# A pair's second masks made one slot later, and the next adjacency loaded behind the rows

## What is computed

```python
mask = adjacency + eye > 0                      # first network, the same for its 3 layers
for l in range(3):
    scores = leaky(si[:, :, None] + sj[:, None, :] + attn_b[l])
    attn = softmax(where(mask, scores, -inf))
    h = layernorm(x + attn @ x)
    x = layernorm(h + gelu(h @ W1[l] + b1[l]) @ W2[l] + b2[l])
# second network, 8 heads: the mask is adjacency > 0
att = softmax(where(A > 0, leaky(a_src + a_dst + b), NEG_INF))
out = relu(att @ xh)
```

## Time and profile before

| | |
|---|---|
| median of 3 runs | 2313.42 us (2313.23 to 2313.54) |
| the profiled execution, its own time | 2312.53 us |
| span from its first to its last instruction | 2310.8 us |
| TensorE busy (matmul) | 2213.7 us, 96% of the span |
| VectorE busy | 1809.3 us, 78% |
| ScalarE busy | 1684.7 us, 73% |
| mean granted TensorE clock | 0.985 of full |

### The profile page before, as it was taken

How to read it: one execution, slowest core, us unless ns; L and a number is a source line. 1 busy time by engine, 2 the same in 40 slices (tenths; PEclk the granted TensorE clock), 3 DMA queues, 4 the chain that set the end, 5 groups by cost and what they waited for, 6 DMA issues and landing times.

```text
span 2310.8 us, 32320 instructions
## 1 busy us (share of the span) xinstructions
PE 2213.7 (96%) x10501; PEld 1560.7 (68%) x10501; DVE 1809.3 (78%) x5722; ACT 1684.7 (73%) x3243; POOL 201.1 (9%) x200
## 2 busy tenths in 40 slices
PE   5999999999999999999999999999999999999976
PEld 3766767767766777676676667766776776777643
DVE  5566687878788788887788797887878877766777
ACT  2444468777877768777787778787787877888786
POOL 0010110010100110001100101000100011001100
PEclk9999999999999999999999999999999999999978
DMA  6011025333172242432353430632415322200111
GB/s 221 10 37 55 10 96 158 106 115 124 28 219 87 74 142 78 155 124 65 109 154 97 137 119 29 203 107 73 135 53 184 110 64 93 69 19 19 37 42 37
DMA packets 115874, 219.30 MB, mean 95 GB/s; under 512 B 7768, under 2 KB 57212, under 8 KB 110332
## 3 DMA queue, kind: packets, MB, share of 16 engines
q1 hardware_dynamic: 115708, 217.24, 29.8%
HBM read 164.52 MB, written 52.69 MB: 94 GB/s over the span
## 4 chain that ended last, share of the span: by engine, by line
PE 79%; DVE 13%; ACT 4%; issue 2%; POOL 1%; DMA 0%; DVEq 0%; POOLq 0%; ACTq 0%
PE ffn L1246 22%; PE av L1163 14%; PE ffn L1235 12%; PE av L1235 12%; PE pT L1146 9%; PE av L1187 4%; PE av L1222 2%; DVE prob L778 2%; DVE prob L769 1%; ACT xs L553 1%; POOL rstd L470 1%; DVE lone L730 1%; PE trow L1125 1%; PE av L1273 1%; PE trow L1273 1%
## 5 line engine op out<-in xcount | busy, mean ns | idle before, releaser
L1246 PE MATMUL ffn<-w_sb,G 128*128 128x256 f32 x3072 | 740.5, 381 | 0.0
L1246 PEld LDWEIGHTS ffn<-w_sb,G 128*128 128x128 f32 x3072 | 560.8, 191 | 90.2 <-issue 24.3
L778 DVE CUSTOM_DVE_ANT_0 prob<-trow,mask 128x512 f32<-128x512 f32 x676 | 439.0, 685 | 34.3 <-PE trow L1125 19.5
L1146 PEld LDWEIGHTS pT<-ident,prob 128*128 128x128 f32 x2032 | 256.4, 144 | 147.6 <-issue 101.5
L1235 PE MATMUL ffn<-hT,w_sb 128*128 128x512 f32 x768 | 355.0, 595 | 0.9 <-issue 0.9
L1235 PE MATMUL av<-hT,w_sb 128*128 128x512 f32 x768 | 353.8, 593 | 0.0
L470 POOL TENSOR_TENSOR rstd<-veps,mhalf 128x4 f32<-128x4 f32 x127 | 167.2, 1317 | 2071.9 <-DVE veps L713 2071.9
L513 ACT ACTIVATE prob<-prob,s 128x512 f32<-128x512 f32 x484 | 331.5, 715 | 2.4 <-DVE nm L785 1.8
L1146 PE MATMUL pT<-ident,prob 128*128 128x128 f32 x2032 | 312.3, 278 | 19.8 <-DVE prob L841 7.5
L519 ACT ACTIVATE prob<-prob,nm 128x512 f32<-128x512 f32 x448 | 317.6, 712 | 0.0
L1163 PE MATMUL av<-xs,prob 128*128 128x257 f32 x1024 | 244.3, 380 | 3.9 <-ACT prob L524 3.9
(11 more groups left out here) (154 smaller groups left out, 2727.2 us busy)
## 6 DMA issues: line engine op xcount, KB each, us to landing
w_sb<-in_L_gnn_W SPq DMA_DIRECT2D x48, 1024.0 KB, 8.4
blocks_dram<-blocks SPq DMA_DIRECT2D x168, 256.0 KB, 4.2
prob<-blocks_dram SPq DMA_DIRECT2D x42, 1024.0 KB, 4.8
trow<-rows_dram SPq DMA_DIRECT2D x127, 256.0 KB, 3.2
adj_sb<-in_adj SPq DMA_DIRECT2D x16, 1024.0 KB, 7.0
xin<-in_x SPq DMA_DIRECT2D x16, 512.0 KB, 6.2
x0r<-in_x SPq DMA_DIRECT2D x16, 512.0 KB, 5.8
out<-o SPq DMA_DIRECT2D x15, 512.0 KB, 3.2
```

What stands on the lines that cost most here:

```text
L778: return v.tensor_tensor_reduce(out=out_[:, t, :], in0=targets, in1=mask[:, t, :], scale=1.0, scalar=LEAST, op0=ALU.add, op1=ALU.max, accu ...
L1146: last = te.transpose(pT[bank][:, j * P:(j + 1) * P], src[:, t, j * P:(j + 1) * P], ident[:])
L1246: last = te.matmul(ffn[part][:, at:at + D], G[:, f, t * P:(t + 1) * P], w2_sb[:, g // 2 % STAGES, f, :], start=f == 0, stop=f == FT - 1)
```

## The change

`make_masks(1)` leaves the end of the slot k = 5. It is called in slot k = 0 of the next pair, between the scores (and `heads_out`, where there is one) and `first_targets`. In seven slots, those with k = 0 and p from 1 to 7, it thus stands directly ahead of the first instructions that read the mask. The masks of the very first pair are made ahead of the loop, as before. On the queue of SyncE, the wait for s_masks and the load of the next pair's first adjacency leave the head of the slot k = 0 and stand behind both x loads, the weights and the rows of the slot's second head.

```diff
                 if k == 0 and not last:
-                    sp.wait_ge(s_masks, 2 * p + 2)
-                    load_adj(2 * p + 2)
                     sp.wait_ge(s_av0e, (SLOTS * p + 1) * T)
                     load_x(2 * p + 2)
...
                 for q in new[1:2]:
                     load_rows(q + 1)
+                if k == 0 and not last:
+                    sp.wait_ge(s_masks, 2 * p + 2)
+                    load_adj(2 * p + 2)
...
                 if four is not None:
                     heads_out(four)
+                if k == 0 and p:
+                    make_masks(1)
                 first_targets(s2)
...
                 if k == SLOTS - 1:
                     keep_masks(1)
-                    if p < PAIRS - 1:
-                        make_masks(1)
```

## The result

The changed kernel takes 2353.49 us (median of 4 runs, 2352.40 to 2354.38), the kernel before 2313.32 us beside it; the ratio is 1.0176 with a 95% interval of 1.0160 to 1.0192. It is slower by 40.2 us, inside the range and 4.5 us above the forecast. The profiled execution took 2352.40 us with a span of 2350.6 us, which is 39.8 more than before.

What follows compares the result with a forecast made beforehand. The prediction took TensorE, busy 96% of the span, as the bound. It summed 2312.53 + 28.7 (masks on the chain) + 7.4 (clock) = 2348.6 us, the median 0.9 above, and said 2349, range 2340 to 2361.

Steps and rivals of the forecast that it cites:

- The price of the old place: Masks ending k = 5 delay the closing sum, so TensorE's row of targets is 0.75 us late in six slots: 4.6 us.
- the rival (c): VectorE's idle time takes up the masks and only the gain is left: 2308.8 us; chance 0.04.
- The masks on the chain: In k = 0, g = 12 to 42, s_nm0 comes 3.76 us later (6.38 less 2.62): 22.6 us over six slots.
- Both waits of TensorE: In the six slots, 3.3 us before piece 3 for the eighth gelu, then some 1.2 us for the first probability.
- Slot 6: Nothing is won ahead of it; s_nm0 is 6.3 us later, of which 6.1 us arrive.
- Nothing gives it back: Behind the new waits no TensorE idle time in slot 18 recovers the loss; VectorE and ScalarE shift with it.
- The clock: TensorE's clock falls around the new waits: 0.8 us in each of six slots, 2.6 in slot 6, 7.4 us in all.
- stretches of 0.50 behind each of these waits: Sign expected in the profile: TensorE's granted clock at 0.50 behind each of line 1246's seven waits, 3.3 and 5.5 us.
- The rival (a): TensorE's clock does not fall, because work surrounds the waits: 2342.1 us; chance 0.18.
- (b): Clock falls are long, two to three lengths in every slot, 18 to 28 us: 2360 to 2370 us; chance 0.11.
- The queue: On SyncE the adjacency load moves about 30 us later; its reader comes over two slots later, so cost is nothing.
- (d): Change does not act as written, for instance masks wait for the adjacency or the queue stands: above 2360 us; chance 0.03.

Runs made afterwards that it cites:

- the kernel without masks: Changed kernel without make_masks(1) in the loop, later second graphs using graph 1's masks, waits and loads kept: 2307.12 us, ratio 0.9973 to the kernel before.
- the filler: Changed kernel plus eight unread matmuls (3.4 us) in front of piece 3 in slots k = 0 behind the first pair: 2343.50 us.
- both single halves: Two kernels: the changed kernel with SyncE's old queue order, 2353.04 us; the kernel before with only the adjacency load moved behind the rows, 2312.73 us.
- The split kernel: Changed kernel with the masks cut in two, 3.9 us at the end of k = 5, 2.5 us ahead of the targets: 2317.14 us.
- the gelu ahead: Changed kernel with ScalarE's eighth gelu ahead of all four scores in slots k = 0 behind the first pair: 2340.59 us.
- the version that beats both: Kernel before, masks in place, but their adjacency reduction done early at the ends of k = 0 and k = 4: 2302.13 us, ratio 0.9953.

## Why the prediction was right, point by point

**The price of the old place** was put at 0.75 us in each of six slots. The direction was right, the size a bit small: without the masks slot 18 takes 45.3 us, 1.0 less than before. The wait at line 1125 isn't all that a late start costs: the row of targets started 12.1 us into the slot before and 11.2 without the masks, 0.9 apart, `attend` 22.1 and 21.1. The view's idle time understates such a delay, since it counts from the modelled end of a matmul group, which reaches over the start of the next (1.88 us long, the next 1.72 behind its start). So the bound of the rival (c), 2308.8, was too high by some 1.5 us, and the 2307.1 of the kernel without masks lies below it. In the sum of the prediction the 0.75 doesn't count by itself: it went by the chain, 6.38 - 2.62.

**The masks on the chain** were put at 6.38 - 2.62 = 3.76 us later for s_nm0. Measured: 20.43 - 16.43 = 4.0, and six slots of 50.3 for 46.3, 24 us for the predicted 22.6. The duration of the masks was right (848.88 to 855.22, 6.3). What was left out is small: from the masks' first instruction to the targets it is 6.56 us for 6.38, since `first_targets` waits 0.21 us behind the masks' last instruction, a result of its own engine; and the closing sum starts 0.28 behind TensorE's next slot instead of 0.20. Both waits of TensorE are where they were said to be: 3.71 for 3.3, 0.79 for 1.2, 4.5 together as predicted. The 0.79 shows only in the two slots at full clock; in the others slower work fills it.

**Slot 6**: 6.1 predicted. With its clock's share taken off it is an estimated 6.3: 47.7 (with the filler), less 1.6 (a fall at its end, which in the kernel without masks cost 41.4 - 39.8), less 39.8.

**Nothing gives it back**: right. The slots k = 1, 2, 3 and 5 from slot 7 on have the length they had.

**The clock** was put at 7.4 us, 0.8 for each of the six and 2.6 for slot 6. Measured in the seven slots against the filled ones: 7.1. The spread was not right: 1.7, 0, 1.9, 0, 1.9 and 0.6 in the six, 6.0 in all for the 4.8 predicted, and 1.1 in slot 6 for 2.6. In slot 6 the fall had the 6.8 us that were forecast, but half of it lay over idle time: TensorE was busy for 3.36 of the 6.80 us (last section). So the sum is right by luck in part: two terms were off by 1.2 and 1.5 us, against each other. The sign "stretches of 0.50 behind each of these waits" didn't come either, since slots 18 and 30 have none. The rival (a), no falls, is shown wrong by the filler. Of (b), long falls, three slots had the two-length form, and it cost 1.8 there instead of the 2.6 and more that (b) took: 0.9 to 1.2 us of each fall lay over the first wait, and the slower work took up the second wait of 0.8.

**The queue** at nothing: right, by both single halves.

**What is left.** Between the sum for the profiled execution, 2348.6, and its 2352.40 lie 3.8 us: to within rounding 1.4 from the chain in six slots, 0.2 from slot 6, less 0.3 for the clock behind the new waits, 1.6 from the second fall in slot 6, less 1.5 for the one that slot 3 lost, 1.3 in the slots k = 4, 1.5 at the end, less 0.6 at the start. The 1.3 are slots 10, 28 and 40, in which the row of targets starts 0.2 to 0.3 us later into the slot than before. What delays it there, and what lengthened the end, was not traced to a cause. The rest of the 4.5 us is the step from the profiled execution to the median and the rounding down to 2349.

**The other rivals.** (c) was named with its point of decision, 2.62 us. The split kernel tests it: with 2.5 us and the 0.2 us of the own-result wait, slot 18 takes 46.5, 0.2 more than before. (d) did not occur: line 730 of the profile after waits for the adjacency once, 5.3 us at the start of the kernel, and nowhere in the loop.

## What to carry to other kernels

Idle time of an engine is a place for work only where it lies behind everything of that slot that others wait for. Here VectorE had 7.0 us free at the end of a slot and next to nothing ahead of the targets. Moving 6.4 us into "the slot with room" at the wrong side of that line cost 4.0 us a slot, its full length less the 2.6 us that the slot starts earlier; moving 2.7 us to the right side of it made the kernel faster. Before a move, look for what the in-order list of the next engine keeps behind the waiting instruction, but cost it by the chain: when that one thing, the gelu, was set free, the wait of 3.7 us moved on and only 0.9 of it came back.

## What the hardware showed that was not expected

**The clock's falls follow no simple length of the wait.** Slot 3 has a wait of 2.46 us in both kernels; before, the clock fell to 0.50 (1.2 GHz) in it, after, it did not. Slot 3 in the profile after, columns as in the earlier trace rows:

```profile
164.40:204.70 40.30, 37.83 (x158) 27.01 (x157) 27.44 (x91) 16.41 (x24) 4.31 (x3) 1.00 0.00 0
```

It took 41.7 us with the fall and takes 40.3 without, for the same work. All nine kernels here have the same TensorE work and the same wait of 2.5 us in that slot. Four of their profiles show the fall in it (before, only the queue changed, the gelu ahead, the version that beats both) and five don't. Slots 12, 18 and 42 of the profile after have the same work for TensorE and the same wait of 3.7 us, and had a fall of 6.8 us, none, and one of 3.4. The first line is slot 6 with its wait of 5.5, the others are the three slots (columns as in the table of the seven slots):

```profile
305.50:312.30 6.80, 3.36 (x10) 0.50 0.00 1
582.00:588.80 6.80, 5.56 (x17) 0.50 0.12 29
859.50:866.30 6.80, 5.16 (x29) 1.00 0.09 34
1967.80:1971.20 3.40, 3.40 (x14) 0.50 0.01 4
```

In slot 6 the wait of 1.97 us in front of the transposes of the state did nothing before; in the kernel without masks, where that slot has the same waits, the clock fell behind it:

```profile
322.25 1.34 PE L1225 MATMUL av<-ident,xs 128*128 128x128 f32 x8 [1.98 <-ACT xs L554]
...
323.00:326.40 3.40, 3.40 (x12) 2.77 (x10) 0.53 (x4) 3.40 (x6) 0.00 (x0) 0.50 0.85 328
```

and the slot took 41.4 us instead of 39.8. For these waits of 2 to 4 us the length doesn't decide whether the clock falls, and no run here shows what does; a sum can only carry an average for it: here 7.1 us over seven waits, 1.0 each. The Trainium skill (TensorE: Matmul & The Clock Gate, section HAM oscillation — how this bites in real kernels) tells of falls behind every wait of a loop; here two of six equal waits had none.

**Useless work can be faster than waiting.** Filling six waits of 3.7 us and one of 5.5 with matmuls whose result nobody reads took 10 us off the kernel, 7.1 of them in the slots with the filler. It is a probe and no cure: the kernel that shortens the chain is 41 us faster still.
